# Queries and outputs of a unit leave PSUM in one operation of two banks per engine, in a windowed-attention and FFN layer on one core

## What is computed

```
x = x + attn(layernorm(x), wq, wk, wv, wo)
x = x + ffn(layernorm(x), weight, bias)

attn: 16 query heads, 4 key/value heads, head size 128
      scores = q @ k.T / sqrt(128)
      mask   = (k <= q) & ((k < 4) | (k >= q - 31))      # 4 sinks, window of 32
      out    = softmax(scores) @ v;  return out @ wo.T
ffn:  x_q = round(x / x_scale), w_q = round(weight / w_scale), both int8
      return (x_q @ w_q.T) * x_scale * w_scale + bias
```

## Time and profile before

| | |
|---|---|
| median of 3 runs | 642.61 us (639.35 to 643.13) |
| the profiled execution's own time | 644.98 us |
| its span, first to last instruction | 643.2 us |
| what lies around the span | 1.8 us |
| PE matmul busy | 605.2 us, 94% |
| DVE busy | 544.1 us, 85% |
| ACT busy | 401.3 us, 62% |
| POOL busy | 307.7 us, 48% |
| mean granted TensorE clock | 0.981 |
| chain that ended last, by engine | PE 88%, DVE 5%, ACT 3% |

### The profile page before, as it was taken

The page is one execution under the profiler, slowest core; times in us unless marked ns, Lnnn a source line. Parts: engine busy times, 40 slices in busy tenths (PEclk is TensorE's granted clock), DMA queues, the critical chain, the costliest instruction groups (busy, mean ns, idle before and its releaser), DMA issues.

```text
span 643.2 us, 18268 instructions
## 1 busy us (share of the span) xinstructions
PE 605.2 (94%) x7586; PEld 532.2 (83%) x7586; DVE 544.1 (85%) x1081; ACT 401.3 (62%) x633; POOL 307.7 (48%) x302
## 2 busy tenths in 40 slices
PE   4777999999999999999999999999999999999783
PEld 3456888989898888989898888989898888988772
DVE  3767699989898998989898998989898998979875
ACT  4675775766666666667666666667666666656640
POOL 1132345356554646456464646455564646445530
PEclk9878999999999999999999999999999999999987
DMA  8921310202121121302121121202021121203000
GB/s 283 354 55 47 80 54 12 89 5 82 34 61 57 48 71 19 99 4 82 34 64 55 49 69 26 91 5 85 30 65 53 49 71 27 91 4 92 23 18 33
DMA packets 35714, 41.33 MB, mean 64 GB/s; under 512 B 5808, under 2 KB 26288, under 8 KB 35632
## 3 DMA queue, kind: packets, MB, share of 16 engines
q1 hardware_dynamic: 35632, 40.16, 20.8%
HBM read 10.26 MB, written 4.19 MB: 22 GB/s over the span
## 4 chain that ended last, share of the span: by engine, by line
PE 88%; DVE 5%; ACT 3%; issue 1%; DMA 1%; POOL 0%; SPq 0%; POOLq 0%; ACTq 0%; DVEq 0%
PE ps L532 26%; PE ps L408 25%; PE ps L435 7%; PE ps L384 7%; PE ps L375 6%; PE ps L491 5%; PE ps L514 4%; PE ps L515 4%; ACT mag L680 1%; PE ps L365 1%; DMA small<-in_L_attn_wv 1%; PE ps L559 1%; PE ps L328 1%; PE ps L547 1%; ACT PT L727 0%
## 5 line engine op out<-in xcount | busy, mean ns | idle before, releaser
L408 PE MATMUL ps<-xT,WqT 128*128 128x256 f16 x1536 | 182.0, 276 | 0.6 <-DVE WoT L982 0.4
L532 PE MATMUL ps<-WoT,pool 128*128 128x256 f16 x1536 | 179.8, 274 | 2.5 <-DVE X L901 2.4
L408 PEld LDWEIGHTS ps<-xT,WqT 128*128 128x128 f16 x1536 | 148.7, 99 | 19.1 <-issue 0.9
L532 PEld LDWEIGHTS ps<-WoT,pool 128*128 128x128 f16 x1536 | 148.4, 98 | 19.4 <-issue 2.5
L751 ACT ACTIVATE pool<-ps 128x512 f16<-128x512 f32 x128 | 69.5, 594 | 87.7 <-PE ps L515 87.7
L1171 POOL TENSOR_TENSOR small<-E,rr 128x576 f32<-128x576 f32 x63 | 72.6, 1152 | 106.3 <-DVE rr L888 106.3
L711 ACT ACTIVATE Qs<-ps 128x576 f16<-128x576 f32 x128 | 82.6, 646 | 48.3 <-PE ps L408 48.3
L1177 POOL TENSOR_TENSOR PP<-small,PP 128x576 f16<-128x576 f32 x63 | 80.9, 1283 | 65.6 <-ACT PP L744 65.6
L869 DVE TENSOR_TENSOR Qs<-ps,Qs 128x576 f16<-128x576 f32 x128 | 92.8, 725 | 7.2 <-ACT Qs L711 7.1
L1163 POOL TENSOR_TENSOR Sm<-Sm,mx 128x576 f32<-128x576 f32 x64 | 73.7, 1152 | 43.5 <-DVE mx L879 42.3
L893 DVE SCALAR_TENSOR_TENSOR pool<-ps,pool 128x512 f16<-128x512 f32 x128 | 81.9, 681 | 4.3 <-ACT pool L751 4.3
(11 more groups left out here) (110 smaller groups left out, 883.8 us busy)
## 6 DMA issues: line engine op xcount, KB each, us to landing
VW<-Vn SPq DMA_DIRECT2D x48, 120.0 KB
big<-Vn SPq DMA_DIRECT2D x48, 120.0 KB
X<-in_L_attn_x SPq DMA_DIRECT2D x16, 256.0 KB, 7.4
out<-pool SPq DMA_DIRECT2D x14, 256.0 KB, 2.3
VW<-Vn SPq DMA_DIRECT2D x48, 60.0 KB
big<-Vn SPq DMA_DIRECT2D x48, 60.0 KB
big<-in_L_attn_wq SPq DMA_DIRECT2D x4, 512.0 KB, 8.5
pool<-in_L_attn_wo SPq DMA_DIRECT2D x4, 512.0 KB, 9.0
```

The source lines that it names most:

```text
L408: a = pe.matmul(banks[BANK_Q[f]][:, j * 256:j * 256 + 256], WqT[:, k, wl, h * 128:h * 128 + 128], xT[:, b % 2, k, xl, :], start=(n == 1), ...
L532: a = pe.matmul(banks[BANK_OUT][:, t * 256:t * 256 + 256], OT[:, p, ol, h, t * 128:t * 128 + 128], WoT[:, 4 * g + h, wl, :], start=first, ...
```

## The change

The views of the queries and of the outputs now cover both banks. `q_high`, `q_low`, `o_high` and `o_low` become one instruction per unit on their engine in place of two: 128 x 1152 for the queries and 128 x 1024 for the outputs. The output tile OT gets the order (half, head, query), so that the merged write is contiguous. Semaphores that counted banks now count units. In the loop the merged q_high(t+1) stands behind exps(t), and the merged q_low(t+1) behind probs(t). What stood ahead of exps and of probs is gone.

```diff
-        def q_views(p, f):
-            src = bass.AP(ps, 512 * BANK_Q[f], [[4096, 128], [256, 2], [STEP, NT], [1, 32]])
-            dst = [bass.AP(Qs, ((p * 2 + l) * NT * 128) + 64 * f, [[4 * NT * 128, 128], [32, 2], [128, NT], [1, 32]])
-                   for l in range(2)]
+        def q_views(p):
+            src = bass.AP(ps, 512 * BANK_Q[0], [[4096, 128], [256, 4], [STEP, NT], [1, 32]])
+            dst = [bass.AP(Qs, (p * 2 + l) * NT * 128, [[4 * NT * 128, 128], [32, 4], [128, NT], [1, 32]]) for l in range(2)]
...
-        def o_view(j):
-            return banks[BANK_O[j]][:, :].rearrange("p (h q) -> p h q", h=4), slice(128 * j, 128 * j + 128)
+        def o_views(u):
+            src = ps[:, BANK_O[0]:BANK_O[1] + 1, :].rearrange("p j n -> p (j n)")
+            return src, [OT[:, u % 2, l].rearrange("p j h q -> p (j h q)") for l in range(2)]
...
             def q_fill(u, f):
-                if u:
-                    pe.wait_ge(q_l, 2 * (u - 1) + f + 1)
+                if u and f == 0:
+                    pe.wait_ge(q_l, u)
...
             def scores(u):
-                pe.wait_ge(q_l, 2 * u + 2)
+                pe.wait_ge(q_l, u + 1)
...
                 if u:
-                    pe.wait_ge(o_l, 2 * u + j - 1)
+                    pe.wait_ge(o_l, u)
...
-            def q_high(u, f):
-                src, dst = q_views(u % 2, f)
-                act.wait_ge(q_ps, 2 * u + f + 1)
+            def q_high(u):
+                src, dst = q_views(u % 2)
+                act.wait_ge(q_ps, 2 * u + 2)
                 act.activation(dst[0], src, ACT.Copy).then_inc(q_h, 1)
...
                 if back:
-                    o_high(t - 2, 0)
-                    o_high(t - 2, 1)
-                q_high(t + 1, 0)
+                    o_high(t - 2)
                 exps(t)
-                q_high(t + 1, 1)
+                q_high(t + 1)
...
                 if back:
-                    o_low(t - 2, 0)
-                    o_low(t - 2, 1)
-                q_low(t + 1, 0)
+                    o_low(t - 2)
...
                 probs(t)
-                q_low(t + 1, 1)
+                q_low(t + 1)
```

More of the change, by code:

```diff
@@ L126, in build @@
         PT = sb("PT", [128, 2, 1024], F16)
-        OT = pool16[:, 0:4096].rearrange("p (u l h t) -> p u l h t", u=2, l=2, h=4)
+        OT = pool16[:, 0:4096].rearrange("p (u l j h q) -> p u l j h q", u=2, l=2, j=2, h=4)
         st2 = sb("st2", [128, 2, 6], F32)
@@ L351, in wo_transpose @@
                 pe.wait_ge(ld_o[g], 16)
-                pe.wait_ge(q_l, 2 * (g + 2) + 2)
+                pe.wait_ge(q_l, g + 3)
                 w_transpose(f"o{g}", wo32[:, g, :])
@@ L520, in out_proj @@
                 p = u % 2
-                pe.wait_ge(o_l, 2 * u + 2)
+                pe.wait_ge(o_l, u + 1)
                 if b == 0:
@@ L531, in out_proj @@
                             end = h == 3 and t == 1 and n == 2
-                            a = pe.matmul(banks[BANK_OUT][:, t * 256:t * 256 + 256], OT[:, p, ol, h, t * 128:t * 128 + 128],
+                            a = pe.matmul(banks[BANK_OUT][:, t * 256:t * 256 + 256], OT[:, p, ol, t, h, :],
                                           WoT[:, 4 * g + h, wl, :], start=first, stop=(end and g == KV - 1),
@@ L572, in ffn_weights @@
                 a.then_inc(wf_ps, 1)
-                pe.wait_ge(q_l, 2 * 9 + 1)
+                pe.wait_ge(q_l, 10)
                 pe.matmul(banks[0][:, 0:256], ones[:, :], diag[:, :, :].rearrange("p t o -> p (t o)"),
@@ L744, in p_high, with o_high @@
                 act.activation(PP[:, p, :, 0, :], Pn[:, p], ACT.Copy).then_inc(p_h, 1)
[L746 to L749, removed]
+            def o_high(u):
+                src, dst = o_views(u)
+                act.wait_ge(o_ps, 2 * u + 2)
+                if u > 1:
                     act.wait_ge(out_ps, u - 1)
-                act.activation(OT[:, u % 2, 0, :, cols], src, ACT.Copy, scale=1.0 / P_UP).then_inc(o_h, 1)
+                act.activation(dst[0], src, ACT.Copy, scale=1.0 / P_UP).then_inc(o_h, 1)
             weight_sum(0, am[:, 4:5], small[:, 0, :], ld_k)
@@ L764, in _ @@
             k_high(0, 0)
-            q_high(0, 0)
-            q_high(0, 1)
+            q_high(0)
             ln_split(1)
@@ L815, in _ @@
             p_high(u - 1)
-            o_high(u - 2, 0)
-            o_high(u - 2, 1)
-            q_high(u + 1, 0)
+            o_high(u - 2)
             exps(u)
-            q_high(u + 1, 1)
+            q_high(u + 1)
             pt_evac(u - 1)
@@ L823, in _ @@
             exps(u + 1)
-            o_high(u - 1, 0)
-            o_high(u - 1, 1)
+            o_high(u - 1)
             pt_evac(u)
             p_high(u + 1)
-            o_high(u, 0)
-            o_high(u, 1)
+            o_high(u)
             pt_evac(u + 1)
-            o_high(u + 1, 0)
-            o_high(u + 1, 1)
+            o_high(u + 1)
             ffn_t_evac(B - 2)
@@ L864, in v_low, with q_low @@
                 dve.tensor_tensor(Vn[:, t, 1, :], banks[v_bank(b, t)][:, :], Vn[:, t, 0, :], ALU.subtract).then_inc(v_l, 1)
-            def q_low(u, f):
-                src, dst = q_views(u % 2, f)
-                dve.wait_ge(q_h, 2 * u + f + 1)
+            def q_low(u):
+                src, dst = q_views(u % 2)
+                dve.wait_ge(q_h, u + 1)
                 dve.tensor_tensor(dst[1], src, dst[0], ALU.subtract).then_inc(q_l, 1)
@@ L888, in probs, with o_low @@
                 dve.reciprocal(rr[:, p, :], sg[:, p, :]).then_inc(p_r, 1)
[L890 to L894, removed]
+            def o_low(u):
+                src, dst = o_views(u)
+                dve.wait_ge(o_h, u + 1)
+                dve.scalar_tensor_tensor(dst[1], src, 1.0 / P_UP, dst[0], ALU.mult, ALU.subtract).then_inc(o_l, 1)
             def ffn_residual(b):
@@ L1035, in _ @@
             maxima("q")
-            q_low(0, 0)
-            q_low(0, 1)
+            q_low(0)
             ln_norm(1)
@@ L1104, in _ @@
             s_max(u)
[L1105 to L1108, removed]
+            o_low(u - 2)
+            q_low(u + 1)
             probs(u)
@@ L1118, in _ @@
                               ALU.mult).then_inc(p_dve, 1)
-            o_low(u - 1, 0)
-            o_low(u - 1, 1)
+            o_low(u - 1)
             dve.wait_ge(p_h, NU)
@@ L1123, in _ @@
             ffn_out(B - 3)
-            o_low(u, 0)
-            o_low(u, 1)
+            o_low(u)
             ffn_norm(B - 2)
             ffn_quant(B - 2)
-            o_low(u + 1, 0)
-            o_low(u + 1, 1)
+            o_low(u + 1)
             ffn_residual(B - 1)
```

## The result

The changed kernel takes 668.84 us (median of 4 runs, 667.82 to 670.95) against 642.79 us before (median of 4). The ratio on record is 1.0418 (the quotient of the two medians is 1.0405), with a 95% interval of 1.0391 to 1.0445, so it is about 4% slower. Its profiled execution took 670.95 us with a span of 669.2, 26.0 us more than that of before by either figure.

What follows compares the result with a forecast made beforehand. PE, busy without waits in the steady part, was taken as the bound. Loop 21.3, tail 2.0 and start 0.5 make 23.8, say 24 us, on 642.6: 667 us, range 649 to 679.

Steps and rivals of the forecast that it cites:

- What the merging saves: PE issues the same matmuls; merged outputs stand where ACT and DVE wait for exps anyway, so costed at 0.
- Rival 1: Each merged operation saves a fixed part, about 0.11 us on DVE, similar on ACT: 661 us, chance 0.08.
- The cost behind the reciprocal: On DVE, merged q_low takes 1.25 us to the next instruction instead of 0.61, so what follows is 0.64 later.
- First cycle: First four-unit cycle: DVE and ACT lateness delays pt_evac, and scores of unit 30 wait 0.4 us.
- The echo: Lateness from unit 29 returns through ACT, DVE and POOL, so s_shift of unit 31 (D) comes 0.6 us late.
- Settled: Later cycles: s_max of unit 32 (A) 1.5 us late; the next two units' scores wait 0.9 and 1.0, sum 1.9.
- The loop's sum: Twelve four-unit cycles, the first at 0.4 us and 11 at 1.9, make 21.3 us.
- The tail: Last four units: merged queries arrive about 1.0 us later, once for unit 61 and once for 63: 2.0 us.
- The start: At the kernel's start the merged q_high ends 0.5 us later in a chain of ACT: 0.5 us.
- Rival 2: No echo: L914 keeps ahead of POOL's L1177, or unit 31's s_shift delay stays under 0.3 us; 650 us, chance 0.15.
- Rival 3: The cover holds, PE never waits, and saved busy time counts only at the ends: 641 us, chance 0.06.
- Rival 4: TensorE's clock falls with the waits, each of 22 costing 1.7 us more: 704 us, chance 0.03.

Runs made afterwards that it cites:

- e1: The kernel before with only the outputs merged (o_high, o_low), the queries still in halves at their old places: 643.11 us against 642.83, ratio 1.0008.
- e5: The kernel before, nothing merged, but both halves of q_high(t+1) behind exps(t) and both of q_low(t+1) behind probs(t): 671.57 us, ratio 1.0461.
- e9: Against the kernel before, only queries merged, q_high ahead of exps (tail too) and q_low ahead of probs in the loop; outputs in halves: 647.63 us, ratio 1.0088.
- e3: The kernel before, nothing merged, ACT untouched; on DVE the first half of q_low(t+1) moved from before probs(t) to behind it: 668.73 us, ratio 1.0407.
- e4: The changed kernel with its merged q_high(t+1) moved ahead of exps(t) and q_low(t+1) ahead of probs(t) in the loop: 649.14 us, ratio 1.0115.
- e2: The changed kernel with its outputs in halves again, so only the queries merged: 667.51 us, ratio 1.0390.
- e8: The changed kernel with ACT's pt_evac(t-1) moved ahead of k_high or v_high and x_evac: 685.02 us, ratio 1.0670.
- e10: The changed kernel with POOL's ffn_store moved from ahead of p_norm(t) to behind it: 663.47 us, ratio 1.0307.

## Why the prediction was right

The forecast was 667 us (649 to 679), the measurement is 668.84. Its steps, one by one:

- **What the merging saves: 0.** Nearly right. PE's matmuls are the same, and in the loop e1 shows no effect of the outputs. On DVE the next operation follows 1.22 us after the merged one, which is 2 x 0.61 as the rows of before gave it; two halves that stand together take 1.28 (e5). On ACT it is 1.01 (340.07 to 341.08 in the changed kernel) against 1.06. Rival 1 had 0.11 us or more saved on each, 0.5 us per cycle: e5 puts the whole gain of both engines at 0.25.
- **The cost behind the reciprocal, 0.64 us by 1.25.** Measured 1.22, so 0.61. ACT's 1.03 was 1.01.
- **First cycle, 0.4.** The first loss of the loop behind unit 10 is 0.61 us, in unit 13, and alone in its cycle, as walked.
- **The echo, s_shift of D 0.6 late.** It comes 3.14 us after the start of the scores of unit 31 (338.20 against 335.06) and came 2.61 after it before (327.26, the scores at 324.65): 0.5 late.
- **Settled: s_max of A 1.5 late, waits of 0.9 and 1.0.** s_max is 1.4 late, the units are 0.88 and 0.97 longer.
- **The loop's sum, 21.3.** Measured 20.2: ten full cycles and two partial ones, not eleven and one.
- **The tail, 2.0.** On the way to the scores of units 61 and 63, 0.93 and 1.08 are lost, though of the 0.93 only 0.57 is a wait for the queries. Behind them another 1.4 us is lost, which had no term. Of it 0.8 is the outputs', which I had put at 0: the end of the kernel from the first pv behind out_proj on takes 28.45 us in every kernel with merged outputs and 27.65 in every one without, to 0.01, since pv (L514) waits there for o_low. The other 0.6 is out_proj, 5.01 us against 4.45, which varies (e9). At L532, the place that I had named as a sign, PE waits 0.42 us for o_low in unit 60, against 0.16 before.
- **The start, 0.5.** No such loss shows; what there is lies within the scatter of the first units.
- **A term was missing, between units 6 and 10: 3.5 us.** Two of them are the wait at L575. `ffn_weights` waits there for the queries of unit 9. Before, the first half was enough (`2 * 9 + 1`), and it stood ahead of the sum; the merged kernel can only wait for all of them, behind the reciprocal:

```profile
124.89 0.70 PE L575 MATMUL ps<-diag,ones 128*128 128x256 f32 x2 [1.99 <-DVE Qs L861]
```

  The prediction had no term for this wait. The larger part of it is the order's and not the count's: e5, which waits for the first half alone, has 1.39 us there, and e3, also for the first half, 2.44, where before had none. e4 waits for all, but ahead of the sum, and has 1.08. Most of the rest stands ahead of it: a wait of 1.02 us for pt_evac at the scores of unit 8. DVE does the pieces of the FFN's weights in step 6 (L997 to L1001 of the changed kernel, 108.0 to 109.35 us) and is late there, which I take for the reason without having tried it.

So the total is right with errors in it that cancel in part: 3.5 us missing at units 6 to 10 and 1.4 behind the tail, against 1.1 too much in the loop and 0.5 at the start. Without the start the losses of the profile are 27.1 us, where I had 23.3; the medians differ by 26.0. The mechanism and the loop's size were foreseen; that the total came within about 2 us of the forecast is in part luck.

Rival 2 (no echo, 650 us) fell on the margin that it named: the second L905 did not get through, it takes 1.69 us with its partner. Rival 3 (the cover holds) fell with the result, e2 and e3. Rival 4 did not occur in the loop: PE's granted clock is 1.00 from 160 to 520 us with waits of 0.7 and 0.8 us at the scores. At single places the clock did fall in some profiles: in e2, e8 and e10 behind the wait at L575, so that e2 and e10 lose 5.2 us between units 6 and 10 where the changed kernel, with the same wait of 1.99 us and its clock unchanged, loses 3.5. The rule of the Trainium skill on fixed costs ("VectorE: DVE Perf Modes", "The TRN2 errata — SBUF-src ops pay a fixed extra latency per instruction") agrees roughly with the busy times, 0.15 us less for the pair on DVE and 0.18 on ACT against the estimates of 0.125 and 0.143, and not with the distances from start to start, 0.06 and 0.05 less by e5, which are what counts in a queue.

No variant beat the kernel before. With PE busy without a gap from 160 to 560 us there, e1 is as fast, and the others are slower. What keeps e4 and e9 about 6 us longer is located above, almost all of it at the ends; why DVE brings o_low late to out_proj in step 6 was not tried and stays open.

## What to carry to other kernels

When two operations are merged, look first at what stood between them: here the first half filled the wait for the exponentials, and the merged one stands wholly behind it. An engine with some per cent of slack on average can have none in three units of four, so walk the whole period, with each queue's fixed order, before calling a delay hidden. And the operation that the bound engine waits for need not be the late one: moving pt_evac ahead cost 16 us more.

## What the runs showed of the hardware

- DVE's tensor_scalar operations from SBUF to SBUF wait for POOL's long operation to end, and the hold goes both ways: POOL's L1160 took 1.44 us in place of 1.28 where the first L905 ran over its start. I had expected only the first. In the changed kernel the second L905 got through only with L1160's end (the pair took 1.69 us in place of 0.73), and L878 took 0.98 in place of 0.17. The tensor_tensor L861, with one input in PSUM, took 1.30 us beside POOL's L1154, as it does on the mean (1.301).
- Merging two PSUM operations of 576 columns saves 0.15 us of DVE's recorded busy time, but only 0.06 from the start of the pair to the start of the next operation (1.22 us against 1.28 in e5).
- Behind PE's waits in the tail TensorE's clock fell to 1.2 GHz (granted 0.50) in every profile, but what that cost differed with the same waits: behind 1.03 and 2.39 us the same 24 matmuls took 4.24 us in e1, 4.45 before and 5.28 in e3.
